# Attention and deformable convolution of 32 images on one core: another order of stages for ScalarE and VectorE, x loaded first, seam rows copied by ScalarE

## The chip, the cores and the metric

One core of one Trainium2 chip runs the whole program. The metric is the device time of one execution in microseconds, from three runs of the kernel before. All times below are microseconds (us) unless marked ns. The engines are TensorE (PE; its weight loads are shown as PEld), VectorE (DVE), ScalarE (ACT), GpSimd (POOL) and SyncE (SP), which only starts DMAs here; ScalarE starts some DMAs too.

## What is computed

The input x is 32 images of 192 channels and 32 x 32 positions in fp32. Two layers are added to it one after the other, each on a group-normalized input:

```python
def attention(x, w_qkv, w_out, b_out):              # B=32, C=192, N=1024
    q, k, v = split(einsum('bnc,dc->bnd', tokens(x), w_qkv))
    attn = softmax(einsum('bcn,bdn->bcd', q, k) * 48 ** -0.5)   # over channels
    return einsum('bnc,dc->bnd', attn @ v, w_out) + b_out

def deformable(x, ...):                             # 3 x 3 taps
    offset = clip(conv(x, off_w, off_b), -8, 8)     # 18 channels
    mask = 2 * sigmoid(conv(x, mask_w, mask_b))     # 9 channels
    y = deform_conv(x, offset, mask, proj_w, proj_b)     # bilinear samples
    return gelu(batchnorm(y) * gamma + beta)        # mean and variance over all images

x = x + attention(groupnorm(x))
x = x + deformable(groupnorm(x))
```

## The kernel before

**Two parts per image.** `part0` makes everything that an image needs before its deformable convolution, in stages with names: statistics of x (`x_stats`), `moments0`, `group0`, `rstd0`, the normalization (`norm0` to `norm3`, ScalarE) with its fp16 high and low parts (`low0` to `low3`, VectorE), the turning of x into tokens (`turn_x0` to `turn_x3`), the Gram matrix (`gram`), its products (`gram_wq`, `logits`), softmax over channels (`exp`, `prob`), `prob_wo`, `wv`, the product with x (`apply0` to `apply3`, which gives x1), then the same normalization of x1 (`moments1`, `group1`, `rstd1`, `norm4` to `norm7`, `low4` to `low7`) into the fp16 planes `x2`, the copies for taps that look left and right (`x2s`, by DMA), and from there offsets, mask and the bilinear weights ("hats") of rows (`rows`, `row_act`, `row_hats`) and of columns (`columns`, `column_hats`).

**`part1`** is the deformable convolution. It runs 48 units `u` per image. A unit on TensorE is: `turn_s(u+2)`, three fp32 transposes of a sampling matrix sT (line 765) into the PSUM banks `sps`; `convolve(u)`, nine fp16 products of sh and sl with zh and zl (lines 782 to 784); `z_group(u+10)`, five products of the projection weights with `x2` (lines 751 to 755) into `zps`. Each of the two PSUM results is cast to fp16 by ScalarE (`split_s` line 987, `split_z` line 963), and VectorE writes what the cast lost (lines 1266 and 1260). GpSimd makes sT as a product of row and column hats (line 1456), one for every two units. `turn_s(u)` waits until `split_s(u-2)` is done on VectorE; `z_group(g)` waits for `split_z(g-2)`. After every sixth unit ScalarE copies the finished accumulator y from `acc` into `ypm` (lines 1007 and 1008), and the next `convolve` waits for that copy. `TURN_Y` and `SCALE_Y` name the units at which y is turned and scaled.

**What sets the order.** Nothing is scheduled by a program. Every engine runs its own list in the order in which the code writes it. The table `PLAN` says beside which unit of `part1` of one image the stages of `part0` of the next image stand; numbers above 47 or below 0 spill into the neighbouring image. `beside` writes these stages at the end of a unit on each engine. So a stage that waits on an engine holds back all the casts behind it on that engine. Images come in a loop of two (`Fori`, line 391), with the first and the last three written out. For image 0 alone, `part0` is run with nothing beside it, and `part1` begins with ten `z_group`s.

**The start.** VectorE waits for the weights of the two convolutions, finds their largest magnitude, scales them to a power of two and splits them into fp16 high and low parts (lines 1035 to 1062), then begins with x. The three attention matrices follow at `turn_x3` (`weights_ready`). SyncE loads the convolution weights, then `eye`, x of image 0 and the tables `avg`, `cy`, `cx`.

**Between `low7` and the offsets.** SyncE starts six shifted copies x2 to x2s and two "seam" copies of three rows each into `x2w` (lines 506 and 507), which the `z_group`s of the first tile read. GpSimd waits for all eight, sets edge columns to zero (`edges`, line 1433) and raises `x2_moved`, on which both the offset convolution (line 694) and `z_group(0)` wait.

Of the kernel before, what the change touches and what calls it, by code (L numbers as in the profile page):

```python
# [35 lines left out]
P = 128  # L36
# [49 lines left out]
def build(nc, x, w_qkT, w_v, w_outT, b_out, w_off, b_off, w_proj, proj_b, gamma, beta,  # L86
# [6 lines left out]
    with ExitStack() as ctx:  # L93
# [33 lines left out]
        boff = sb("boff", [P, TILES, J])  # L127
# [111 lines left out]
        x2_shifted = sem("x2_shifted")  # L239
        edges_due = sem("edges_due")  # L240
# [46 lines left out]
        MATRIX_DMAS = TILES + 3 + 3 + 6 + 3 * 4  # L287
# [55 lines left out]
        def all_pairs(eng, step):  # L343
# [3 lines left out]
            for i in range(PAIRS - ROUND_ENDS):  # L347
# [33 lines left out]
        def images(program, eng):  # L381
# [3 lines left out]
            part0, part1, weights_ready = program  # L385
            for stage in STAGES:
                part0(stage, 0, 0)
                if stage == "turn_x3":
                    weights_ready()
# [25 lines left out]
        TURN_Y, SCALE_Y = (14, 25, 36), (16, 26, 37)  # L415
# [51 lines left out]
        def _(sp):  # L467
# [3 lines left out]

            load_blocks(sp, off_stage, w_off, weights_in)
# [3 lines left out]
            sp.dma_start(avg_sb[:, :, :], avg.rearrange("p (a b) -> p a b", a=4)).then_inc(const_in, 16)  # L476
            sp.dma_start(cy_sb[:, :], cy).then_inc(const_in, 16)
            sp.dma_start(cx_sb[:, :, :], cx.rearrange("p (k x) -> p k x", k=TAPS)).then_inc(const_in, 16)
# [15 lines left out]
            def shift(b, par):  # L494

                seam = lambda h: x2w_all[:, :, par, h * WRAP * W:(h + 1) * WRAP * W]
# [9 lines left out]
                sp.dma_start(seam(0), plane[:, :, N - WRAP * W:N]).then_inc(x2_shifted, 16)  # L506
                sp.dma_start(seam(1), plane[:, :, 0:WRAP * W]).then_inc(x2_shifted, 16)
# [78 lines left out]
        def _(pe):  # L586
            pe.wait_ge(const_in, CONST_DMAS * 16)
            pe.wait_ge(dve_setup, 2)
            pe.wait_ge(pool_setup, 1)

            for i in range(2):
                mm = pe.transpose(yt[:, i * P:(i + 1) * P], wmax[:, i:i + 1].broadcast_to([P, P]), eye32[:, :])
            mm.then_inc(pe_setup, 1)

            def weights_ready():
                pe.wait_ge(matrices_in, MATRIX_DMAS * 16)
                pe.wait_ge(dve_setup, 4)
                for i in range(3):
                    mm = pe.transpose(acc[:, i * P:(i + 1) * P], amax[:, i:i + 1].broadcast_to([P, P]), eye32[:, :])
                mm.then_inc(pe_setup, 1)  # L600
# [26 lines left out]
            def transpose_x(r, b):  # L627
                if r == 0:
                    pe.wait_ge(xn_lo, 8 * b + 4)
# [26 lines left out]
            def gram_times_wq(b):  # L656

                if first(b):
                    pe.wait_ge(dve_setup, 5)
# [168 lines left out]
            def part1(b, par, left, i=None):  # L828
                if first(b) or i is not None:
                    for g in range(AHEAD):  # L830
                        z_group(g, b, par)
                    turn_s(0, b)
                    turn_s(1, b)
# [21 lines left out]
            images((part0, part1, weights_ready), pe)  # L855
# [4 lines left out]
        def _(act):  # L860
# [9 lines left out]
            for t in range(TILES):  # L870
                act.dma_start(boff[:, t, :], b_off.partition_broadcast(P)).then_inc(matrices_in, 16)
            act.wait_ge(const_in, CONST_DMAS * 16)
            act.wait_ge(pool_setup, 1)

# [650 lines left out]
```

## Time and profile before

| | |
|---|---|
| time, median of 3 runs | 3814.17 us (3813.31 to 3821.13) |
| profiled execution | 3809.4 us, of which its span 3807.7 us |
| TensorE busy | 3417.3 us, 90% of the span |
| VectorE, ScalarE, GpSimd busy | 2609.9, 2127.9 and 1427.8 us |
| before the regular run of images | 0 to about 118 us |
| last stage (GELU and final sum, TensorE idle) | about 3592 to 3808 us |
| granted TensorE clock, mean | 0.965 |

The time divides into three stretches. In the first 118 us nothing overlaps, since image 0 is alone. From there to about 3580 us an image takes some 108.5 us and TensorE is busy nearly all of it. The last 216 us load, add and store all images and are bound by DMA. A wait in the rows below is told as "engine line waited for: us in total, times, longest"; in a timeline row the bracket is the idle time just before the instruction and what ended it.

### The profile page before, as it was taken

The numbers are of one execution on the slowest core, as the hardware profiler recorded it, in microseconds if no ns is written. First come the engines' busy times: TensorE is split into PE (matmuls) and PEld (weight loads), VectorE is DVE, ScalarE is ACT, GpSimd is POOL, SyncE is SP. The second block draws the span as 40 slices with busy tenths as digits, with TensorE's granted clock in tenths as the row PEclk, the third lists the DMA queues.
The fourth block names the chain that finished last, engine by engine and source line by source line (L and its number), as shares of the span: only waits on it lengthen the run. The fifth ranks groups of instructions, "written<-read, shape, count | busy, mean of one in ns | idle before, by whom it ended". The sixth has DMA issues, their size and how long they took to land.

```text
span 3807.7 us, 109692 instructions
## 1 busy us (share of the span) xinstructions
PE 3417.3 (90%) x38854; PEld 3019.7 (79%) x38854; DVE 2609.9 (69%) x5727; ACT 2127.9 (56%) x4854; POOL 1427.8 (37%) x1226
## 2 busy tenths in 40 slices
PE   2799999999999999999999999999999999999500
PEld 1688888888888888888888888888888888888500
DVE  4577777777777777777777777777777777776422
ACT  1465555655656556556565566565655665655332
POOL 1343433443434334334344343344433433444211
PEclk8999999999999999999999999999999999999855
DMA  2011111110111111101111111111111111011498
GB/s 68 18 48 48 40 48 48 48 35 28 43 48 39 48 48 47 35 30 41 47 40 48 47 48 37 33 35 48 40 47 48 47 41 34 31 47 36 138 368 298
DMA packets 104140, 225.31 MB, mean 59 GB/s; under 512 B 38432, under 2 KB 64288, under 8 KB 103584
## 3 DMA queue, kind: packets, MB, share of 16 engines
q1 hardware_dynamic: 92832, 191.76, 15.7%
q0 software_dynamic: 7168, 25.17, 1.7%
q8 instruction: 348, 5.70, 0.6%
q14 instruction: 208, 1.70, 0.2%
q10 hardware_dynamic: 3584, 0.97, 0.1%
HBM read 87.36 MB, written 75.50 MB: 43 GB/s over the span
## 4 chain that ended last, share of the span: by engine, by line
PE 76%; issue 6%; ACT 6%; DVE 5%; DMA 4%; ACTq 1%; DVEq 1%; SPq 1%; POOL 0%; POOLq 0%
PE sps L765 12%; PE acc L782 8%; PE acc L784 8%; PE acc L783 8%; PE l L694 5%; PE zps L755 4%; PE zps L751 4%; PE zps L754 4%; PE zps L752 4%; PE zps L753 4%; DMA xn<-x_scratch 2%; PE l L615 2%; DMA out<-x 1%; PE l L636 1%; DVE xhl_b L1133 1%
## 5 line engine op out<-in xcount | busy, mean ns | idle before, releaser
L1456 POOL TENSOR_TENSOR sT<-ay,bx 128x768 f32<-128x768 f32 x768 | 1140.3, 1493 | 1451.8 <-PE sps L765 1444.3
L782 PE MATMUL acc<-zh,sh 128*128 128x192 f16 x4608 | 1134.0, 246 | 28.2 <-ACT ypm L1008 28.2
L784 PE MATMUL acc<-zh,sl 128*128 128x192 f16 x4608 | 1133.6, 246 | 0.0
L783 PE MATMUL acc<-zl,sh 128*128 128x192 f16 x4608 | 1133.6, 246 | 0.0
L1266 DVE TENSOR_TENSOR sl<-sps,sh 128x384 f16<-128x384 f32 x1536 | 847.0, 552 | 349.3 <-ACT sh L987 328.1
L963 ACT CAST zh<-zps 128x288 f16<-128x288 f32 x1536 | 616.9, 402 | 711.9 <-PE zps L755 692.0
L987 ACT CAST sh<-sps 128x384 f16<-128x384 f32 x1536 | 738.5, 481 | 424.4 <-PE sps L765 413.2
L1260 DVE TENSOR_TENSOR zl<-zps,zh 128x288 f16<-128x288 f32 x1536 | 694.1, 452 | 341.6 <-ACT zh L963 333.6
L765 PE MATMUL sps<-eye,sT 128*128 128x128 f32 x4608 | 769.9, 276 | 10.1 <-issue 7.8
L765 PEld LDWEIGHTS sps<-eye,sT 128*128 128x128 f32 x4608 | 546.5, 141 | 81.6 <-issue 23.1
L782 PEld LDWEIGHTS acc<-zh,sh 128*128 128x128 f16 x4608 | 450.7, 98 | 40.3 <-ACT ypm L1008 33.9
L783 PEld LDWEIGHTS acc<-zl,sh 128*128 128x128 f16 x4608 | 450.9, 98 | 16.6
L784 PEld LDWEIGHTS acc<-zh,sl 128*128 128x128 f16 x4608 | 450.9, 98 | 0.0
L751 PE MATMUL zps<-wpr_h,x 128*128 128x288 f16 x1344 | 384.4, 286 | 0.5 <-DVE zl L1260 0.5
L752 PE MATMUL zps<-wpr_l,x 128*128 128x288 f16 x1344 | 384.4, 286 | 0.0
L753 PE MATMUL zps<-wpr_h,x 128*128 128x288 f16 x1344 | 384.4, 286 | 0.0
L754 PE MATMUL zps<-wpr_h,x 128*128 128x288 f16 x1344 | 384.4, 286 | 0.0
L755 PE MATMUL zps<-wpr_l,x 128*128 128x288 f16 x1344 | 384.4, 286 | 0.0
L1440 POOL TENSOR_TENSOR bx<-off,cx_sb 128x576 f32<-128x576 f32 x128 | 154.0, 1214 | 208.2 <-DVE off L1223 208.2
L694 PE MATMUL l<-wof,x2s 128*128 128x54 f16 x4608 | 186.6, 186 | 13.2 <-POOL x2s L1433 13.2
L694 PEld LDWEIGHTS l<-wof,x2s 128*128 128x128 f16 x4608 | 180.7, 96 | 16.3 <-POOL x2s L1433 13.3
L694 PE MATMUL l<-wof,x 128*128 128x54 f16 x2304 | 175.9, 186 | 0.0
(205 smaller groups left out, 5506.0 us busy)
## 6 DMA issues: line engine op xcount, KB each, us to landing
x2s<-x SPq DMA_DIRECT2D x192, 255.8 KB, 2.5
xin<-in_x SPq DMA_DIRECT2D x32, 512.0 KB, 5.2
xin<-in_x SPq DMA_DIRECT2D x64, 256.0 KB, 5.7
x_scratch<-x SPq DMA_DIRECT2D x32, 512.0 KB, 2.7
y_scratch<-ych SPq DMA_DIRECT2D x32, 512.0 KB, 2.7
zh<-y_scratch SPq DMA_DIRECT2D x20, 512.0 KB, 10.6
zl<-x_scratch SPq DMA_DIRECT2D x20, 512.0 KB, 11.4
out<-zh POOLq DMA_DIRECT2D x20, 512.0 KB, 8.8
```

The costliest lines, as they stand in the source:

```text
L694: mm = pe.matmul(o, src[:, row * W:(row + ROWS_T) * W], wof[:, m, k].rearrange("p i j -> p (i j)"), start=(k == 0 and n == 0), stop=(k == ...
L751: pe.matmul(o, at(0), wpr_h[:, 0, ky, n], start=True, stop=False)
L752: pe.matmul(o, at(0), wpr_l[:, 0, ky, n], start=False, stop=False)
L765: mm = pe.transpose(sps[u % 2][:, kx * P:(kx + 1) * P], sT[:, g, kx, c * P:(c + 1) * P], eye32[:, :])
L782: pe.matmul(acc[:, 0:C], s_h, zh[:, j, ky, z], start=start and kx == 0, stop=False)
L783: pe.matmul(acc[:, 0:C], s_h, zl[:, j, ky, z], start=False, stop=False)
L784: mm = pe.matmul(acc[:, 0:C], s_l, zh[:, j, ky, z], start=False, stop=stop and kx == 2)
L963: act.copy(z_piece(zh, g, par), zps[:, g % 2, 0:KO // 2]).then_inc(z_hi, 1)
L987: act.copy(sh[:, u % S_RING].rearrange("p k n -> p (k n)"), sps[u % 2][:, 0:3 * P]).then_inc(s_hi, 1)
L1260: dve.tensor_tensor(z_piece(zl, g, par), zps[:, g % 2, 0:KO // 2], z_piece(zh, g, par), ALU.subtract)\
L1266: dve.tensor_tensor(one(sl), sps[u % 2][:, 0:3 * P], one(sh), ALU.subtract).then_inc(s_lo, 1)
L1456: pool.tensor_tensor(sT[:, p % ST_RING].rearrange("p k (r x) -> p k r x", r=R), a, x_, ALU.mult)\
```

## The change

**The table.** In `PLAN`, `prob_wo` to `group1` move one unit later (16 to 17, ..., 24 to 25) and `rstd1` stands at 26 together with `norm4`. `norm6` and `norm7` move to 30 and 31, `low6` and `low7` to 32 and 33. A new stage `seams0` stands at 34. `rows1`, `row_act1` and `row_hats1` leave the table (44, 45, 46) and are done at units 7, 10 and 11 of the image's own `part1` (`ROWS_1`); `column_hats1` moves from 46 to 44. `TURN_Y` 25 becomes 26, `SCALE_Y` 16 and 26 become 17 and 27; column hats 2 move from unit 14 to 16; y's statistics and the offset distance move by one unit.

**Seams.** ScalarE copies the seam rows at `seams0` in two instructions, after waiting for `low7`. The two seam DMAs are gone, GpSimd waits for six copies, and `z_group(0)` waits for ScalarE (`seams_copied`) and no longer for `x2_moved`.

**Transposes.** `turn_x0` waits for the third low part (`low2`), `turn_x2` for the fourth.

**The start.** SyncE loads x of image 0 first, then the tables, then the weights. VectorE does all weight work inside `part0` of image 0: the maxima and the attention matrices behind `low3`, the scaling of the convolution weights behind `gram_wq0`, their splitting behind `prob0`. The bias `boff` is one DMA and not eight. ScalarE runs one tiny activation as soon as the constants are there. Behind `edges0`, five of the ten first `z_group`s are done, before the offset convolution.

```diff
-        MATRIX_DMAS = TILES + 3 + 3 + 6 + 3 * 4
+        MATRIX_DMAS = 1 + 3 + 3 + 6 + 3 * 4
...
-                21: ("apply3",), 22: ("moments1",), 24: ("group1",), 25: ("rstd1",), 26: ("norm4",),
+                22: ("apply3",), 23: ("moments1",), 25: ("group1",), 26: ("rstd1", "norm4"), 27: ("norm5",),
...
-            load_blocks(sp, off_stage, w_off, weights_in)
-            load_blocks(sp, proj_stage, w_proj, weights_in)
-            sp.dma_start(eye32[:, :], eye).then_inc(const_in, 16)
-            load_x(0)
...
+            load_x(0)
+            sp.dma_start(avg_sb[:, :, :], avg.rearrange("p (a b) -> p a b", a=4)).then_inc(const_in, 16)
...
+            load_blocks(sp, off_stage, w_off, weights_in)
             load_blocks(sp, proj_stage, w_proj, weights_in)
...
-                sp.dma_start(seam(0), plane[:, :, N - WRAP * W:N]).then_inc(x2_shifted, 16)
-                sp.dma_start(seam(1), plane[:, :, 0:WRAP * W]).then_inc(x2_shifted, 16)
...
+                if stage == "edges0":
+                    pe.wait_ge(dve_setup, 4)
+                    for g in range(AHEAD // 2):
+                        z_group(g, 0, 0)
...
-                if r == 0:
-                    pe.wait_ge(xn_lo, 8 * b + 4)
+                if r % 2 == 0:
+                    pe.wait_ge(xn_lo, 8 * b + 3 + r // 2)
...
                 if g == 0:
-                    pe.wait_ge(x2_moved, b + 1)
+                    pe.wait_ge(seams_copied, b + 1)
...
+            act.activation(gb[:, :], mhalf[:, :], ACT.Identity, scale=mhalf[:, 0:1], bias=mhalf[:, 1:2])
...
+                if name == "seams":
+                    act.wait_ge(xn_lo, 8 * b + 8)
+                    for h, row in ((0, H - WRAP), (1, 0)):
+                        at = (PAD_T + row) * W
+                        ins = act.copy(x2w_all[:, :, par, h * WRAP * W:(h + 1) * WRAP * W],
+                                       x2_all[:, :, par, at:at + WRAP * W])
+                    ins.then_inc(seams_copied, 1)
...
-                    if u in (14, 24):
-                        column_hats((14, 24).index(u) + 2, b, par)
+                    if u in (16, 24):
+                        column_hats((16, 24).index(u) + 2, b, par)
+                    if u == ROWS_1[1]:
+                        row_act(1, b, par)
...
+            def first_image(stage):
+                if stage == "low3":
+                    largest_weights()
+                    split_matrices()
+                    powers_of_two(scale[:, :], unscale[:, :], wmaxt[:, :])
+                if stage == "gram_wq0":
+                    for w, shaped, w_h, w_l, i in splits:
+                        dve.tensor_scalar(w, w, scale[:, i:i + 1], None, ALU.mult)
+                if stage == "prob0":
+                    for w, shaped, w_h, w_l, i in splits:
+                        dve.tensor_copy(w_h, shaped)
...
-                pool.wait_ge(x2_shifted, 128 * b + 128)
+                pool.wait_ge(x2_shifted, 96 * b + 96)
```

How the instructions stand before and after is shown at three places. **The start, on VectorE.** `zh` and `zl` hold the raw convolution weights there, `ych` the attention matrices. Before, the program begins so:

```order
L1036 TENSOR_REDUCE wmaxt<-zh 128x1 [waits weights_in]
L1036 TENSOR_REDUCE wmaxt<-zl 128x1
L1038 TENSOR_SCALAR cmid<-cy_sb 128x1 [waits const_in]
...
L1055 TENSOR_SCALAR zl<-zl,scale 128x1728 x2
...
L1061 TENSOR_TENSOR wpr_l<-zl,wpr_h 128x1728 x2
L1106 BN_STATS stats<-xin 128x6 [waits x_loaded] x4
```

After the change:

```order
L1053 TENSOR_SCALAR cmid<-cy_sb 128x1 [waits const_in]
L1054 CAST eye<-eye 128x128
L1122 BN_STATS stats<-xin 128x6 [waits x_loaded] x4
...
L1158 TENSOR_TENSOR xhl_b<-xn,xhl_b 64x512 [waits xn_hi] x2
L1071 TENSOR_REDUCE wmaxt<-zh 128x1 [waits weights_in]
L1071 TENSOR_REDUCE wmaxt<-zl 128x1
...
L1125 SCALAR_TENSOR_TENSOR t_l<-l_1,t_h 64x192
L1106 TENSOR_SCALAR zh<-zh,scale 128x243 x2
L1106 TENSOR_SCALAR zl<-zl,scale 128x1728 x2
L1200 TENSOR_REDUCE nmax<-l_0 128x1 [waits log_ps]
```

The statistics of x now stand ahead of all weight work, and the weight work stands in three pieces behind stages of image 0. **Beside units 13 to 17, on ScalarE**, in a written-out image whose order is that of the loop; bx are the column hats. Before:

```order
L954 ACTIVATE bx<-bx 128x576 [waits dx_sb]
L956 ACTIVATE bx<-bx 128x576
L963 CAST zh<-zps 128x288 [waits z_ps,sz_done]
L987 CAST sh<-sps1 128x384 [waits sz_done,s_ps]
L963 CAST zh<-zps 128x288 [waits z_ps]
L987 CAST sh<-sps0 128x384 [waits sz_done,s_ps]
L963 CAST zh<-zps 128x288 [waits z_ps]
L891 ACTIVATE rmat_h<-l0_1 128x192 [waits r_ps]
```

After the change:

```order
L979 CAST zh<-zps 128x288 [waits z_ps,sz_done]
L1003 CAST sh<-sps1 128x384 [waits sz_done,s_ps]
L979 CAST zh<-zps 128x288 [waits z_ps]
L1003 CAST sh<-sps0 128x384 [waits sz_done,s_ps]
L970 ACTIVATE bx<-bx 128x576 [waits dx_sb]
L972 ACTIVATE bx<-bx 128x576
L979 CAST zh<-zps 128x288 [waits z_ps]
L1003 CAST sh<-sps1 128x384 [waits sz_done,s_ps]
L1025 COPY ypm<-acc 128x192 [waits yt_ps,sz_done]
```

The pair on bx stands two units later, and the copy of y now comes ahead of rmat_h (`prob_wo`). **Beside units 33 to 35, on ScalarE**, in the same image. Before:

```order
L987 CAST sh<-sps0 128x384 [waits sz_done,s_ps]
L963 CAST zh<-zps 128x288 [waits z_ps]
L987 CAST sh<-sps1 128x384 [waits sz_done,s_ps]
L1007 COPY ypm<-acc 128x192 [waits yt_ps,sz_done]
L1008 COPY ypm<-acc 128x64
```

After the change:

```order
L1003 CAST sh<-sps0 128x384 [waits sz_done,s_ps]
L979 CAST zh<-zps 128x288 [waits z_ps]
L949 COPY x2w<-x2 128x3x96 [waits xn_lo]
L949 COPY x2w<-x2 128x3x96
L1003 CAST sh<-sps1 128x384 [waits sz_done,s_ps]
L1025 COPY ypm<-acc 128x192 [waits yt_ps,sz_done]
L1026 COPY ypm<-acc 128x64
```

The two seam copies, with their wait for the last low part, stand ahead of a cast of s and of a copy of y.

## Rows read from the trace of the kernel before

**Rows 1.** Waits of PE in 220 to 3472 us (thirty images): total, times, longest.
```profile
PE acc L782 <- ACT ypm L1008: 26.7, 47, 1.0
PE l L636 <- DVE xhl_b L1133: 24.3, 30, 0.9
PE sps L765 <- issue: 7.8, 13, 0.9
PE l L615 <- DVE prob_l L1095: 7.0, 30, 0.2
```

**Rows 2.** Timeline of PE: start, us, instruction, idle time before; the waits of one image.
```profile
1342.03 0.23 PE L636 MATMUL l<-eye,xh_a 128*128 128x128 f16 x1 [0.81 <-DVE xhl_b L1133]
1367.56 0.26 PE L615 MATMUL l<-wo_h,prob_h 128*128 128x192 f16 x1 [0.24 <-DVE prob_l L1095]
1399.57 0.26 PE L782 MATMUL acc<-zh,sh 128*128 128x192 f16 x1 [0.57 <-ACT ypm L1008]
1437.70 0.26 PE L782 MATMUL acc<-zh,sh 128*128 128x192 f16 x1 [0.52 <-ACT ypm L1008]
```

**Rows 3.** Timeline of DVE, POOL and ACT around the softmax of one image.
```profile
1360.73 1.40 DVE L1180 TENSOR_TENSOR nmaxs<-nmax,log_scale 128x1 f32<-128x1 f32 x2
1365.65 0.16 DVE L1184 RECIPROCAL rinv<-rsum 128x2 f32<-128x2 f32 x1
...
1360.56 1.48 POOL L1456 TENSOR_TENSOR sT<-ay,bx 128x768 f32<-128x768 f32 x1 [5.34 <-PE sps L765]
1364.36 1.48 POOL L1456 TENSOR_TENSOR sT<-ay,bx 128x768 f32<-128x768 f32 x1 [1.21 <-PE sps L765]
...
1363.51 0.69 ACT L954 ACTIVATE bx<-bx 128x576 f32<-128x576 f32 x1
```

**Rows 4.** Timeline of DVE and ACT around the last low part and the copy of y.
```profile
1405.69 1.20 DVE L1133 TENSOR_TENSOR x<-xn,x 64x512 f16<-64x512 f32 x1
...
1409.01 0.32 ACT L1007 COPY ypm<-acc 128x192 f32<-128x192 f32 x1 [0.26 <-PE acc L784]
```

**Rows 5.** Timeline of DVE and PE in the stage of image 0 alone.
```profile
16.28 0.66 DVE L1036 TENSOR_REDUCE wmaxt<-zh 128x1 f32<-128x486 f32 x1 [16.28 <-DMA zl<-in_w_proj]
16.85 3.74 DVE L1036 TENSOR_REDUCE wmaxt<-zl 128x1 f32<-128x3456 f32 x1
23.02 0.15 DVE L1038 TENSOR_SCALAR cmid<-cy_sb 128x1 f32<-128x1 f32 x1 [2.42 <-DMA cx_sb<-in_cx]
25.88 2.15 DVE L1055 TENSOR_SCALAR zl<-zl,scale 128x1728 f32<-128x1728 f32 x2
28.09 0.72 DVE L1058 CAST wof<-zh 128x243 f16<-128x243 f32 x2
35.21 2.46 DVE L1106 BATCH_NORM_STATS2 stats<-xin 128x6 f32<-128x512 f32 x4
50.20 2.00 DVE L1069 TENSOR_REDUCE amax<-ych 128x1 f32<-128x768 f32 x3
59.99 0.47 DVE L1095 SCALAR_TENSOR_TENSOR gram<-l,gram 128x192 f16<-128x192 f32 x2
66.28 0.61 DVE L1175 TENSOR_REDUCE nmax<-l 128x1 f32<-128x192 f32 x2 [2.58 <-PE l L617]
73.36 0.61 DVE L1095 SCALAR_TENSOR_TENSOR rmat_l<-l,rmat_h 128x192 f16<-128x192 f32 x2 [3.15 <-ACT rmat_h L891]
```

**Rows 6.** The chain that ended last: last low parts and offset convolution of image 0.
```profile
96.01 1.30 DVE x L1133 x2
102.50 7.72 PE l L694 x216
```

**Rows 7.** Timeline of ACT: last hats of image 0, first and last of ten z casts.
```profile
115.14 0.44 ACT L945 ACTIVATE ay<-ay 128x288 f32<-128x288 f32 x1 [0.64 <-DVE ay L1227]
117.33 0.68 ACT L963 CAST zh<-zps 128x288 f16<-128x288 f32 x2
...
126.18 0.40 ACT L963 CAST zh<-zps 128x288 f16<-128x288 f32 x1 [0.64 <-PE zps L755]
```

More of the change, by code:

```diff
@@ L587, in _ @@
             pe.wait_ge(const_in, CONST_DMAS * 16)
-            pe.wait_ge(dve_setup, 2)
+            pe.wait_ge(dve_setup, 1)
             pe.wait_ge(pool_setup, 1)
[L591 to L600, printed above, removed]
+            def first_image(stage):
+                if stage == "turn_x3":
+                    pe.wait_ge(dve_setup, 2)
+                    for i in range(5):
+                        column = wmax[:, i:i + 1] if i < 2 else amax[:, i - 2:i - 1]
+                        at = yt[:, i * P:(i + 1) * P] if i < 2 else acc[:, (i - 2) * P:(i - 1) * P]
+                        mm = pe.transpose(at, column.broadcast_to([P, P]), eye32[:, :])
+                    mm.then_inc(pe_setup, 1)
+                if stage == "edges0":
+                    pe.wait_ge(dve_setup, 4)
+                    for g in range(AHEAD // 2):
+                        z_group(g, 0, 0)
             def group_stats(n, b):
@@ L829, in part1 @@
                 if first(b) or i is not None:
-                    for g in range(AHEAD):
+                    for g in range(AHEAD // 2 if i is None else 0, AHEAD):
                         z_group(g, b, par)
@@ L990, in part1 @@
                 if first(b) or i is not None:
-                    for g in range(AHEAD):
+                    for g in range(AHEAD // 2 if i is None else 0, AHEAD):
                         split_z(g, b, par)
@@ L1032, in _ @@
         def _(dve):
-            dve.wait_ge(weights_in, 6 * 16)
-            for i, stage in enumerate((off_stage, proj_stage)):
-                dve.tensor_reduce(wmaxt[:, i:i + 1], stage, AX.XY, ALU.max, apply_absolute_value=True)
             dve.wait_ge(const_in, CONST_DMAS * 16)
@@ L1092, in weights_ready, with first_image, channel_stats @@
                 ins.then_inc(dve_setup, 1)
+            def first_image(stage):
+                if stage == "low3":
[8 more added lines that the diff above has]
+                        dve.tensor_copy(w_h, shaped)
+                    dve.drain()
+                    for w, shaped, w_h, w_l, i in splits:
+                        ins = dve.tensor_tensor(w_l, shaped, w_h, ALU.subtract)
+                    ins.then_inc(dve_setup, 1)
+                    dve.wait_ge(dve_setup, 4)
+                if stage == "edges0":
+                    for g in range(AHEAD // 2):
+                        split_z(g, 0, 0)
+            def channel_stats(q, src):
+                i, half = divmod(q, 2)
+                dve.bn_stats(stats[:, i, half], src[:, i, half * 512:half * 512 + 512])
             def low_part(dst, src, by, hi):
@@ L1336, in part1 @@
                 if first(b) or i is not None:
-                    for g in range(AHEAD):
+                    for g in range(AHEAD // 2 if i is None else 0, AHEAD):
                         split_z(g, b, par)
@@ L1369, in part1 @@
                     y_stats(3, b, par)
-            images((part0, part1, weights_ready), dve)
+            images((part0, part1, first_image), dve)
             def again():
@@ L1463, in part1 @@
                     beside(part0, u, b, par, left)
-            images((part0, part1, lambda: None), pool)
+            images((part0, part1, lambda stage: None), pool)
             where_far(pool, lambda: once_more(
```

138 lines of the change are left out of this document (67 added, 71 removed), and 8 rows, old and new, of the table PLAN.

## The prediction, made before the changed kernel was run

> **What bounds the kernel now.** I read the page first: TensorE is busy 90% of the span, and its idle time lies at both ends. Then the waits of TensorE over thirty regular images [rows 1]: they add up to 65.8 us, so whatever the change does there, it can give back about 2 us per image. Of that, 7.8 us stand as "issue", which the profile ties to no other engine; it occurs every second image only, and I leave it alone. The timeline shows where the others sit [rows 2]. The first transposes of x wait 0.81 for the last low part, in all 30 images. `prob_wo` waits 0.24 for `prob`. `convolve` of unit 30 waits 0.57 for the copy of y, and `convolve` of the next image's unit 0 waits 0.52 for it in the images without the issue wait; 47 such waits are 30 of the first kind and 17 of the second. The second view is the timeline of the stage in which image 0 is alone [rows 5 to 7]; there every microsecond of the chain counts once. The last stage (216 us, bound by DMA) is not touched, and I carry it over.
>
> **Start: x ahead of the weights.** The statistics of x begin at 35.21 [rows 5], behind a wait for the tables that ends at 23.02 and 12.2 us of weight work. Now they begin when x and the tables have landed. The weights, first in the queue, landed at 16.28 with about 2.0 MB; x and the tables have 1.5 MB (both by their shapes). In proportion that is 12 to 13 us, and I take 12.5, with 10 to 15 as bounds. From statistics to the end of the low parts nothing changes (35.21 to 50.20, 15.0 us), so `low3` ends at 27.5, by which time the weights and matrices are there. Then:
> - From 50.20 to the low part of the Gram matrix at 59.99 are 9.8 us: maxima of the three matrices, their turning, the split. Now the maxima of the convolution weights come in too, 0.66 + 3.74 overlapping to 4.3, and for two more maxima 0.8 in small instructions and turning, an estimate. `gram` is then at 27.5 + 9.8 + 4.3 + 0.8 = 42.4, **17.6 us sooner**.
> - Scaling the weights (28.09 less 0.6 ahead of 25.88, 2.8 us) stands ahead of the maximum of the logits, where VectorE idled 2.58: costs 0.2.
> - Splitting them (28.09 to 35.21, 7.1 us) stands ahead of the low part of rmat, where VectorE idled 3.15: **costs 4.0**.
> - From the last low part's end (96.01 + 1.30 = 97.3) to the offset convolution at 102.50 [rows 6] TensorE waited for DMAs and GpSimd. Five `z_group`s now stand there. Ten of them took 117.33 to 126.18 for nine steps [rows 7], 0.98 each, so seam copies and five groups need about 6 us: the convolution starts 0.8 later, but on an engine that has just worked. It took 7.72 for 216 products; I take 5.9 to 7.7, a gain of 1.0 net.
> - After the offsets, the second row half no longer stands ahead of the z casts (115.14 less its 0.64 of idle, to 116.00: 1.5 us), and five of nine steps are gone (4.4): **5.9 sooner**.
> Sum: 17.6 - 0.2 - 4.0 + 1.0 + 5.9 = **20.3 us**, bounds 15 and 25. ScalarE's table load moves off the chain too, worth at most 1.3, within these bounds.
>
> **Transposes on the third low part.** TensorE was ready 0.81 before 1342.03. Two low parts take 1.30 back to back [rows 6], 0.65 each, and here VectorE has two casts' remainders between the third and the fourth (about half a microsecond each, an estimate), so the third is done over 1 us earlier and the whole wait goes: **24.3 us** in thirty images. Nothing is behind it: the next transposes wait for ScalarE as before.
>
> **ScalarE's heavy stages off y's copies.** `norm6` stood a unit ahead of the copy after unit 29, now it stands behind it: 30 x 0.57 = 17.1. `column_hats1` and `row_act1` leave units 45 and 46: the other 17 waits, 26.7 - 17.1 = 9.6, go. `row_act1` now costs ScalarE 0.9 (two of 0.44 [rows 7]) at unit 10, where TensorE has the whole Gram product behind the unit, and VectorE's two row instructions fall into idle time beside units 7 and 11: nothing. Together **26.7 us**.
>
> **`prob_wo` one unit later, column hats from unit 14 to 16.** The wait of 0.24 goes (7.0 us). But what stood between was a cushion. `prob` ran from 1365.65 to about 1367.5 [rows 2, 3]. Without the pair of column hats (two of 0.69) ahead of it on ScalarE it could begin at 1364.5. GpSimd's sT runs there, 1364.36 to 1365.84. In the same image `nmaxs`, a one-column instruction, took 1.3 of the 1.40 of its pair because sT ran from 1360.56; it ended with sT. So `prob`, apart from its reciprocal, is held to 1365.84 and ends at 1367.4 as before. Behind it VectorE has the remainder of s for unit 17 (some 0.55, an estimate), until 1368.0. `turn_s(19)` waits for that, and TensorE, which no longer has `prob_wo` to do at unit 16, is free for it at 1367.3 (1367.56 less the 0.24). A new wait of 0.7, bounds 0 and 1.0: **costs 30 x 0.69 = 20.7**, so the edit costs 13.7 net.
>
> The Trainium skill, page "SBUF — State Buffer", section "Who interferes with whom", says that GpSimd and VectorE share one pair of ports, whole instruction by whole instruction, and that not only instructions with two SBUF inputs but also a `tensor_scalar` in a 2-port mode take it. By that rule both high parts of `prob` are held, as in my sum; if only two-input instructions were, the wait would be near nothing, which is rival B below. The trace agrees for two inputs (`nmaxs`).
>
> **Seam copies on ScalarE.** The trace has no such copy. Its nearest rows are a copy of 192 columns, 0.32 [rows 4], and a cast of 288 columns, 0.40 [rows 7]; two of 288 overlapping make 0.7, bounds 0.6 and 1.6. They stand ahead of the cast of s for unit 37 and of the copy of y after unit 35, and wait for `low7`. `low7` stood at 1405.69 and took 1.20 since an sT held it; a unit later (1.7) it runs free and ends near 1407.8. The copy of y has 0.26 of idle ahead of it [rows 4] and gets behind by 0.6, so `convolve` of unit 36 waits 0.35, bounds 0.1 and 1.3: **costs 30 x 0.35 = 10.5**. The seam DMAs that go were on no path of TensorE in a regular image. `x2_moved` comes earlier relative to `low7`, and `low7` is a unit later: nothing.
>
> **Sum.** Thirty images: 24.3 + 26.7 + 7.0 - 20.7 - 10.5 = 26.8, with image 0 as a thirty-first 27.7. With the start: 20.3 + 27.7 = 48.0 of 3809.4 in the profiled execution, 3761.4. The median of the runs is 4.8 above that execution, so the prediction for the median is **3766**.
>
> **Rivals.**
> - B, no collision at `prob`: VectorE's five instructions run beside sT, `turn_s(19)` does not wait. For it: `prob` was never seen beside sT. Against: `nmaxs`. 31 x 0.69 = 21.4 less: 3745.
> - C, the seam copies cost 0.9 more per image, because they are slow or `low7` is held by sT after all: 31 x 0.9 = 28 more, 3794. The same number comes out if other small waits arise at stages that now meet another neighbour. For it: sT held `low7` and others in the trace; against: sT of that time waits behind `edges`.
> - D, the landing of x and tables is not sooner than 20 us, since ScalarE's loads share the engines: 7.5 us less gain, 3773.
> - E, slower: `low7`, seam copies, cast and copy of y are one chain through two engines at unit 35. Beyond my 0.35 each further microsecond counts fully, thirty-one times; the gain of 48 is gone at 1.55 more per image, and at 1.9 more (copies of 0.8 each, and `low7` a whole sT later) it is 31 x 1.9 - 48 = 11 slower, 3825. It decides only beyond both bounds above together.
>
> **How the numbers follow.** Forecast 0.50, B 0.20, C 0.18, D 0.07, not faster by the change of order at all 0.03 (3810), E 0.02. The range takes in B, C and D with the bounds of the start: 3736 to 3796. A measurement of this kernel tells about 0.2% (8 us) from no change. Faster by more than that: 0.95; within: 0.03; slower: 0.02.
>
> **What would show it.** The statistics of x begin near 12.5, the tenth z cast ends near 106 and not 126. TensorE's wait at the transposes of x is gone; no wait of unit 30 for y; a new wait of 0.7 at sps behind the remainder of s, and one of 0.35 at acc behind the copy of y, each about thirty times. `prob`'s instructions end with sT. It is wrong if the new waits are more than two, or if the images do not come 0.9 closer together.

## The result and the profile after

| | before | after |
|---|---|---|
| median of the runs | 3813.74 us (4 runs, 3804.66 to 3821.13) | 3750.34 us (4 runs, 3740.71 to 3751.09) |
| ratio, 95% interval | | 0.9824, 0.9808 to 0.984 |
| profiled execution | 3809.4 us | 3751.09 us |
| begin of the Gram product of image 1 (TensorE) | 156.37 us | 134.01 us |
| from one Gram product to the next, regular image without a back edge | 108.53 us | 106.91 us |

The change gives 63.4 us where 48.0 were forecast. The time lies inside the range (3736 to 3796), on its lower side. Where it came from is seen in a table of stretches, cut at the begin of image 1's Gram product, at that of the last image, and at TensorE's end. Columns: stretch, its length, busy time and number of instructions of TensorE, its weight loads, VectorE, ScalarE, GpSimd, then the granted clock, the share of the DMA engines, GB/s. Before:

```profile
0.00:156.00 156.00, 69.68 (x696) 52.59 (x696) 71.42 (x157) 44.62 (x85) 34.39 (x33) 0.86 0.20 52
156.00:3413.00 3257.00, 3185.28 (x36382) 2820.77 (x36383) 2369.89 (x5275) 1932.84 (x4494) 1292.24 (x1079) 1.00 0.13 42
3413.00:3579.00 166.00, 162.32 (x1778) 146.32 (x1776) 106.61 (x240) 88.00 (x224) 65.46 (x49) 1.00 0.12 37
3579.00:3807.70 228.70, 0.00 (x0) 0.00 (x0) 61.98 (x58) 62.48 (x53) 35.70 (x65) 0.51 0.93 325
```

After:

```profile
0.00:134.00 134.00, 71.50 (x696) 53.84 (x696) 70.88 (x157) 46.02 (x88) 34.06 (x33) 0.82 0.21 59
134.00:3350.00 3216.00, 3178.40 (x36384) 2825.09 (x36385) 2416.02 (x5270) 1951.19 (x4552) 1284.31 (x1079) 1.00 0.13 41
3350.00:3515.00 165.00, 162.03 (x1777) 146.25 (x1774) 109.11 (x245) 89.50 (x228) 65.13 (x49) 1.00 0.12 38
3515.00:3749.40 234.40, 0.00 (x0) 0.00 (x0) 61.78 (x57) 62.48 (x53) 35.82 (x65) 0.51 0.93 317
```

The start is 22 us shorter, the thirty images 41, the last one 1. The last stage, whose code is the same, took 5.9 longer in this execution, counted from TensorE's end (229 us before, where I had put 216; 227 to 241 us in the executions profiled below, over all kernels). TensorE is therefore done 64.2 sooner (3578.45 against 3514.23), while the two profiled executions differ by 58.3 only. In the thirty images VectorE is busy 46 us longer with the same work, because other instructions of it now take longer, among them the scaling in `prob` (30 x 0.97 = 29 us more, looked at below) and the offset distance (`ypos`, 53.6 us and not 14.3). Only the first has a wait of TensorE behind it.

**The regular images.** The waits of TensorE from 200 to 3412 us, in the columns of [rows 1]:

```profile
PE sps L765 <- DVE sl L1295: 22.8, 41, 1.1
PE acc L782 <- ACT ypm L1026: 9.3, 30, 0.4
PE l L615 <- DVE rmat_l L1125: 0.4, 1, 0.4
```

Of the four rows in [rows 1] those for the low parts (24.3) and for `prob` (7.0) are gone, the one for y fell from 26.7 in 47 waits to 9.3 in 30, and one at `sps` is new. It holds two things. Thirty of its 41 waits are of 0.5 and stand 17.7 us behind the Gram product; a timeline there:

```profile
1326.14 1.48 POOL L1489 TENSOR_TENSOR sT<-ay,bx 128x768 f32<-128x768 f32 x1 [1.20 <-PE sps L765]
...
1326.27 0.15 DVE L1209 RECIPROCAL rinv<-rsum 128x2 f32<-128x2 f32 x1
...
1326.51 1.14 DVE L1211 TENSOR_SCALAR rinv<-rinv 128x2 f32<-128x2 f32 x1
...
1327.72 0.54 DVE L1215 TENSOR_SCALAR prob_h<-xt,rinv 128x192 f16<-128x192 f32 x2
...
1328.35 0.74 DVE L1125 SCALAR_TENSOR_TENSOR prob_l<-xt,rinv,prob_h 128x192 f16<-128x192 f32 x2
...
1329.01 0.54 DVE L1295 TENSOR_TENSOR sl<-sps,sh 128x384 f16<-128x384 f32 x1
...
1329.61 0.55 PE L765 MATMUL sps<-eye,sT 128*128 128x128 f32 x3 [0.51 <-DVE sl L1295]
```

This is the collision of the forecast. The scaling of two numbers takes 1.14 us and ends at 1327.65, just behind sT (1327.62); the reciprocal ahead of it, also inside sT, takes 0.15. `prob` ends at 1329.09, the remainder of s behind it at 1329.55, and TensorE starts 0.06 later.

The wait for y stands at unit 36 alone:

```profile
1369.23 0.69 DVE L1158 TENSOR_TENSOR x<-xn,x 64x512 f16<-64x512 f32 x1
...
1369.96 0.76 ACT L949 COPY x2w<-x 128x288 f16<-128x288 f16 x2 [0.35 <-DVE x L1158]
...
1371.00 0.32 ACT L1025 COPY ypm<-acc 128x192 f32<-128x192 f32 x1
...
1371.21 0.23 ACT L1026 COPY ypm<-acc 128x64 f32<-128x64 f32 x1
...
1371.49 0.26 PE L782 MATMUL acc<-zh,sh 128*128 128x192 f16 x1 [0.30 <-ACT ypm L1026]
```

`low7` runs free (0.69), the pair of seam copies takes 0.76, and behind it come the cast of s and the copy of y.

**The end of the loop body.** The other 11 waits at `sps` stand 87 to 88 us behind the Gram product, at the end of the loop body's second image. The fourteen passes of the loop have 13 back edges, so two are without such a wait. The row puts them down to VectorE:

```profile
1504.36 0.56 DVE L1295 TENSOR_TENSOR sl<-sps,sh 128x384 f16<-128x384 f32 x1
...
1505.20 0.55 DVE L1295 TENSOR_TENSOR sl<-sps,sh 128x384 f16<-128x384 f32 x1
...
1506.73 0.54 PE L765 MATMUL sps<-eye,sT 128*128 128x128 f32 x3 [1.14 <-DVE sl L1295]
```

Both remainders had ended by 1505.75, 0.98 before TensorE went on. The kernel before has the same gap in the same place, 0.84 there and called "issue":

```profile
1546.22 0.54 PE L765 MATMUL sps<-eye,sT 128*128 128x128 f32 x3 [0.84 <-issue]
```

**The start.** VectorE's rows of image 0 (below them the last z cast on ScalarE), to be read against [rows 5, 7]:

```profile
11.31 2.46 DVE L1122 BATCH_NORM_STATS2 stats<-xin 128x6 f32<-128x512 f32 x4
...
23.68 1.29 DVE L1158 TENSOR_TENSOR xhl_b<-xn,xhl_b 64x512 f16<-64x512 f32 x2 [0.97 <-ACT xhl_b L885]
...
25.58 3.74 DVE L1071 TENSOR_REDUCE wmaxt<-zl 128x1 f32<-128x3456 f32 x1
...
39.65 0.48 DVE L1125 SCALAR_TENSOR_TENSOR gram<-l,gram 128x192 f16<-128x192 f32 x2
...
46.88 0.61 DVE L1200 TENSOR_REDUCE nmax<-l 128x1 f32<-128x192 f32 x2
...
54.11 3.82 DVE L1112 TENSOR_TENSOR wpr_l<-zl,wpr_h 128x1728 f16<-128x1728 f32 x2
...
57.96 0.61 DVE L1125 SCALAR_TENSOR_TENSOR rmat_l<-l,rmat_h 128x192 f16<-128x192 f32 x2
...
80.54 1.29 DVE L1158 TENSOR_TENSOR x<-xn,x 64x512 f16<-64x512 f32 x2 [0.97 <-ACT x L885]
...
104.11 0.40 ACT L979 CAST zh<-zps 128x288 f16<-128x288 f32 x1 [0.80 <-PE zps L755]
```

And the five z groups and the offset convolution, as stretches (columns as above):

```profile
82.70:88.30 5.60, 5.53 (x27) 3.21 (x28) 1.47 (x4) 1.60 (x4) 0.94 (x2) 0.55 0.25 94
88.30:93.90 5.60, 5.60 (x219) 5.58 (x218) 0.83 (x3) 0.40 (x1) 0.00 (x0) 1.00 0.02 6
```

The groups run at a granted clock of 0.55, the lower of the two levels (1.2 GHz) in the main; the convolution behind them at 1.00 (2.4 GHz) and in 5.60 us. Before, it began on an idle engine and took 7.72 [rows 6].

### The profile page after: what moved, and what is told of

It is laid out like the page before. It is cut to its first block, busy times and chain, and to the rows that moved or that the text cites. A ratio compares the mean times of both kernels' runs of the same rounds, so it can differ in the third digit from the quotient of the medians.

```text
span 3749.4 us, 109745 instructions
## 1 busy us (share of the span) xinstructions
PE 3411.9 (91%) x38854; PEld 3025.2 (81%) x38854; DVE 2657.8 (71%) x5727; ACT 2149.2 (57%) x4919; POOL 1419.3 (38%) x1226
## 4 chain that ended last, share of the span: by engine, by line
PE 82%; DVE 4%; DMA 4%; ACT 3%; issue 3%; DVEq 1%; ACTq 1%; SPq 1%; POOL 0%; POOLq 0%
PE sps L765 13%; PE acc L782 9%; PE acc L784 9%; PE acc L783 9%; PE l L694 5%; PE zps L755 4%; PE zps L751 4%; PE zps L753 4%; PE zps L754 4%; PE zps L752 4%; DMA xn<-x_scratch 3%; PE l L615 2%; DMA out<-x 2%; PE l L636 1%; PE l L617 1%
```

## The experiments

Each kernel is the changed one with the edit shown. "Period" is the distance between two Gram products in regular images that have no wait at the back edge; it repeats within 0.01 us and is therefore a finer measure than the time. Medians with an interval are from three or more rounds against the kernel before, whose median was 3812.89 to 3816.21 us in them.

| kernel | median, us | ratio to before (95%) | image 1 begins | period |
|---|---|---|---|---|
| before | 3813.74 | | 156.37 | 108.53 |
| changed kernel | 3750.34 | 0.9808 to 0.984 | 134.01 | 106.91 |
| start alone | 3799.66 | 0.993 to 0.997 | 139.10 | 108.51 |
| `prob` at 15 | 3731.39 | 0.9768 to 0.9801 | 133.37 | 106.17 |
| column hats at 14 | 3758.86 | 0.9838 to 0.9871 | 132.34 | 107.09 |
| seam copies at 35 | 3733.65 | 0.9776 to 0.9809 | 133.34 | 106.43 |
| four images in the loop | 3747.32 | 0.9804 to 0.9837 | 133.90 | 106.91 |
| splitting spread | 3747.72 | 0.9806 to 0.9838 | 129.10 | 106.91 |
| fourth low part | 3782.6, one run | | 133.38 | 107.88 |
| seam copies twice | 3775.6, one run | | 133.25 | 107.73 |
| three edits | 3711.37 | 0.9713 to 0.9753 | 128.36 | 105.70 |
| five edits | 3705.82 | 0.9699 to 0.9726 | 126.94 | 105.69 |
| seams by DMA | 3726.7, one run | | 137.83 | 106.43 |
| weights first | 3765.4, one run | | 142.65 | 106.91 |

**Start alone.** The table, `TURN_Y`, `SCALE_Y`, the second row half, column hats, seams and transposes are those of before; of that edit the core:

```diff
-                34: ("seams0",), 36: ("edges0",),
+                32: ("low7",), 36: ("edges0",),
...
-                    pe.wait_ge(seams_copied, b + 1)
+                    pe.wait_ge(x2_moved, b + 1)
...
-                if r % 2 == 0:
-                    pe.wait_ge(xn_lo, 8 * b + 3 + r // 2)
+                if r == 0:
+                    pe.wait_ge(xn_lo, 8 * b + 4)
```

> Only the changes of the start are in this kernel (x and tables loaded ahead of the weights, weight work inside image 0, one DMA for the bias, table load moved, five z groups ahead of the offset convolution). The table of stages, the seam DMAs and the wait of the transposes are those of the kernel before. Theory 1 (the surplus over the forecast lies in the thirty images): a regular image takes 108.5 us as before, the Gram product of image 1 begins some 21 to 22.5 us sooner than 156.4, and the median is 21 to 23 below that of before, about 3791 to 3793. Rival (the surplus of 10 to 15 us lies in the start and the first images): 30 to 35 below, about 3781. A gain under 18 would say that the new order has its share in the first image.

It gained 16.5 (3816.21 to 3799.66), and image 1 begins 17.3 sooner. My theory said 21 to 22.5, so it missed, and so did the rival with 30 or more: the surplus is not in the start. Image 1 begins 5.1 us later than in the changed kernel. Three of them are in this row:

```profile
85.78 0.40 PE L754 MATMUL zps<-wpr_h,x2w 128*128 128x288 f16 x1 [13.27 <-POOL x2s L1469]
```

Without ScalarE's copies, z group 0 waits for `x2_moved` (GpSimd's edge columns), so the five groups stand ahead of the convolution on the chain and not beside the DMAs: they begin at 85.78 and not at 82.78. Another 1.6 us lie between the end of the convolution and the last z cast (11.9 and not 10.3). The second row half, which this kernel leaves where it was, stands ahead of the casts there again, so my 21 to 22.5 counted a gain that this kernel does not have.

**`prob` beside unit 15.**

```diff
-                10: ("gram0",), 11: ("gram_wq0",), 12: ("logits0",), 13: ("exp0",), 14: ("prob0",),
+                10: ("gram0",), 11: ("gram_wq0",), 12: ("logits0",), 13: ("exp0",), 15: ("prob0",),
```

> The changed kernel with stage prob beside unit 15 and not 14, nothing else. Theory 1 (prob's instruction on two sums is held by GpSimd's product sT, which runs from 14.2 to 15.7 us after the start of the Gram product): at unit 15 prob meets no sT, its second instruction takes about 0.17 us and not 1.14, TensorE's wait for the remainder of s (0.5 in the row) falls to 0.2 or less, a regular image takes 106.3 to 106.5 and not 106.9, and the time is 11 to 17 below the changed kernel, about 3736. Rival (VectorE simply has too much to do in two units, whoever holds it): the wait moves by a unit and stays 0.4 to 0.6, 106.9 per image, about 3750.

```profile
1322.01 0.17 DVE L1211 TENSOR_SCALAR rinv<-rinv 128x2 f32<-128x2 f32 x1
```

and from its waits of TensorE, 220 to 3400 us:

```profile
PE sps L765 <- DVE sl L1295: 8.0, 10, 1.1
```

The same instruction, one unit later and beside no sT, takes 0.17. The thirty waits are gone, only ten at the back edge are left in the row, and the period falls by 0.74, more than I expected: 19 us, by one number in the table. VectorE's load is the same, so the rival falls.

**Column hats 2 beside unit 14.**

```diff
-                    if u in (16, 24):
-                        column_hats((16, 24).index(u) + 2, b, par)
+                    if u in (14, 24):
+                        column_hats((14, 24).index(u) + 2, b, par)
```

> The changed kernel with the pair of column hats 2 back beside unit 14, nothing else. Theory 1: prob then starts about 1 us later, behind sT, and its instructions run unheld; it ends some 0.2 us later than in the changed kernel, so TensorE's wait behind it is 0.5 to 0.8 in the row and an image takes 106.9 to 107.2: about 3750 to 3758. That is, moving the hats was worth nearly nothing, since the collision ate it. Rival (the later hats do free prob and the wait of 0.5 is only what is left): with the hats back the wait is longer by the pair, 1.2 or more, an image takes 107.6 or more, about 3770.

```profile
1325.14 1.48 POOL L1489 TENSOR_TENSOR sT<-ay,bx 128x768 f32<-128x768 f32 x1 [1.21 <-PE sps L765]
...
1326.66 0.17 DVE L1211 TENSOR_SCALAR rinv<-rinv 128x2 f32<-128x2 f32 x1
...
1328.80 0.55 PE L765 MATMUL sps<-eye,sT 128*128 128x128 f32 x3 [0.70 <-DVE sl L1295]
```

`prob` now comes behind sT, runs free, and ends no sooner: TensorE waits 0.70 and not 0.51, the period is 0.18 longer. Taking the pair of hats (1.4 us) out of its way was worth 0.18.

**Seam copies beside unit 35**, behind the copy of y:

```diff
-                34: ("seams0",), 36: ("edges0",),
+                35: ("seams0",), 36: ("edges0",),
```

> The changed kernel with the seam copies beside unit 35 and not 34, so that they stand behind ScalarE's copy of y and not ahead of it. Theory 1: the wait of 0.31 at acc goes (0.36 from start to start), no other arises, since the next cast of s had 0.4 us of idle and its remainder is wanted a unit later; an image takes 106.5 to 106.6, about 3740. Rival (the seam copies cost wherever they stand, because ScalarE has 0.76 more to do): a wait of about the same size at sps or zps one or two units on, 106.9 per image, about 3750.

```profile
PE sps L765 <- DVE sl L1295: 19.9, 37, 1.1
PE l L615 <- DVE rmat_l L1125: 0.4, 1, 0.4
```

The row at `acc` is gone, nothing takes its place, and the period falls by 0.48, where I had put the wait at 0.36 from start to start: that value was too small. It was the place of the copies, not the work.

**Four images in the loop.**

```diff
-            with nc.Fori(1, NB - 4, 2, engines=[eng.engine], hint_back_edge=True) as b:
-                part1(b, 1, 2)
-                part1(b + 1, 0, 2)
+            with nc.Fori(1, NB - 4, 4, engines=[eng.engine], hint_back_edge=True) as b:
+                for n in range(4):
+                    part1(b + n, 1 - n % 2, 2)
```

> The changed kernel with four images in the loop and not two: seven back edges and not fourteen, the order of all instructions otherwise the same. The wait in question is TensorE's at sps, 87 to 88 us after the start of the Gram product, in 11 of the images at the end of the loop body, 0.4 to 1.3 each; the trace puts it down to VectorE's remainder of s. Theory 1 (it is the back edge of the loop, as the issue wait was before, and VectorE had ended before): it now comes at every fourth image only, at most 7 times, and the time is 3 to 6 shorter, 3744 to 3747. Rival (VectorE is late there, as the row says): it stays at every second image and nothing changes, 3750.

```profile
PE sps L765 <- DVE sl L1295: 15.4, 30, 0.5
PE acc L782 <- ACT ypm L1026: 8.9, 29, 0.4
PE acc L784 <- issue: 3.2, 1, 3.2
```

(Waits of TensorE from 220 to 3400 us, as in the other experiments below and above.) Exactly the thirty waits behind `prob` are left at `sps`, at 0.5 each; the 11 are gone, also at the six back edges that remain. So they belong to the loop and not to VectorE, and 22.8 - 15.4 = 7.4 us of the row were wrongly labelled. But one stall of 3.2 is new, in the first `convolve` behind the loop's exit, and that image takes 111.93: 3.4 later through the stall, and 1.7 more because the granted clock behind it is 0.66 from 3217 to 3222 us (1.00 ahead of it). The median gained 3 us (3750 to 3747), within what the measurement can tell. Why the shorter body has no such stall at its exit stays open.

**Splitting of the weights spread** over VectorE's idle time:

```diff
-                if stage == "gram_wq0":
+                if stage == "gram0":
                     for w, shaped, w_h, w_l, i in splits:
                         dve.tensor_scalar(w, w, scale[:, i:i + 1], None, ALU.mult)
-                if stage == "prob0":
+                if stage == "gram_wq0":
+                    dve.drain()
                     for w, shaped, w_h, w_l, i in splits:
                         dve.tensor_copy(w_h, shaped)
+                if stage == "prob0":
                     dve.drain()
-                    for w, shaped, w_h, w_l, i in splits:
+                    for w, shaped, w_h, w_l, i in splits[:3]:
+                        dve.tensor_tensor(w_l, shaped, w_h, ALU.subtract)
+                if stage == "prob_wo0":
+                    for w, shaped, w_h, w_l, i in splits[3:]:
                         ins = dve.tensor_tensor(w_l, shaped, w_h, ALU.subtract)
```

> The changed kernel with the work on the convolution weights in image 0 put into VectorE's idle stretches: scaling behind gram0, the high parts behind gram_wq0, three of the four low parts behind prob, the last one behind prob_wo. Theory 1 (the splitting in one piece holds the low part of rmat, 4.0 us as forecast): the low part of rmat begins at 53.9 to 54.5 and not 57.96, TensorE's wait for it falls from 5.3 to 1.3 to 1.9, image 1 begins 3.5 to 4.2 sooner (129.8 to 130.5), and the time is about 3746. Rival (what follows is bound by something else, for example by the offset convolution's DMAs): image 1 begins less than 1 sooner, 3750.

```profile
53.46 0.61 DVE L1130 SCALAR_TENSOR_TENSOR rmat_l<-l,rmat_h 128x192 f16<-128x192 f32 x2 [0.46 <-ACT rmat_h L898]
```

The low part of rmat begins 4.5 sooner (57.96 to 53.46), and image 1 4.3 sooner than in the other kernels with the changed start (129.10 against 132.3 to 134.0, mostly some 133.4; the changed kernel itself 134.01). In the median it is 2.6, under what can be told.

**Fourth low part.**

```diff
-                if r % 2 == 0:
-                    pe.wait_ge(xn_lo, 8 * b + 3 + r // 2)
+                if r == 0:
+                    pe.wait_ge(xn_lo, 8 * b + 4)
```

> The changed kernel with the transposes of x waiting for the fourth low part again. Theory 1 (this wait is worth in the changed order what it was before, 0.81 in the row, 0.97 from start to start): an image takes 107.8 to 107.9, in all 29 to 30 us longer, about 3780. Rival (the later stages around it moved, so that part of the wait would have gone anyway): 107.4 or less, 3765.

```profile
PE l L636 <- DVE xhl_b L1158: 24.3, 30, 0.9
```

The old row is back to the tenth (24.3 in 30), and the period grows by 0.97, not by the 0.81 of the row. That difference is looked at below.

**Seam copies twice**, the same two again behind a drain of ScalarE:

```diff
+                    act.drain()
+                    act.copy(x2w_all[:, :, par, 0:WRAP * W], x2_all[:, :, par, PAD_T * W + (H - WRAP) * W:PAD_T * W + H * W])
+                    ins = act.copy(x2w_all[:, :, par, WRAP * W:2 * WRAP * W], x2_all[:, :, par, PAD_T * W:(PAD_T + WRAP) * W])
                     ins.then_inc(seams_copied, 1)
```

> The changed kernel with the two seam copies done twice, one after the other (the same rows again), beside unit 34. Theory 1 (copies, cast of s and copy of y are one chain, and beyond it each further microsecond counts fully): 0.76 more work and a drain of ScalarE make the wait at acc 1.1 to 1.2 and not 0.31, an image takes 107.7 to 107.8, about 25 us longer in all, 3775. Rival (ScalarE's idle time takes it up): wait under 0.7, less than 10 us longer.

```profile
PE acc L782 <- ACT ypm L1029: 32.8, 29, 1.2
```

The waits grow from 0.31 to 1.13 each, the period by 0.82, for 0.76 of copies and the drain. It is one chain and each further microsecond counts: rival E's mechanism is right, though its size never came about.

**Three edits, and five.** The three are `prob` at 15, seam copies at 35, splitting spread; the other two are the loop of four and a call of `largest_conv`, the first half of `largest_weights` (maxima of the convolution weights, with their wait), ahead of the low parts:

```diff
+                if stage == "norm1":
+                    largest_conv()
                 if stage == "low3":
                     largest_weights()
```

> Three edits together on the changed kernel: prob beside unit 15, seam copies beside unit 35, splitting of the convolution weights spread over VectorE's idle stretches. Theory 1 (the three waits are separate, so the gains add): 0.74 and 0.48 less per regular image give 105.7, image 1 begins at about 129, no wait of TensorE is left in a regular image but the one at the back edge; 28 x 1.22 + 4.2 = 38 below the changed kernel, about 3711 to 3716. Rival (ScalarE or VectorE is next in line once both waits are gone): 106.0 or more per image, 3722 or more.

> As the kernel with the three edits, and two more: four images in the loop, and in image 0 the maxima of the convolution weights taken ahead of the low parts, where VectorE waits for ScalarE. Theory 1: the waits at the back edge go and one stall of some 5 us at the loop's exit comes (2 to 5 less in all); the low part of the Gram matrix begins 3 us sooner. Together 4 to 8 below that kernel, 3705 to 3710. Rival (the stall at the exit eats what the edges give, and the maxima meet another wait): within 2 of it.

The gains add: 0.74 + 0.48 = 1.22, and the period is 105.70 (1.21 less). With the five edits there is no wait in a regular image, and TensorE's waits from 220 to 3380 us are two (the stall behind the loop's exit, and one in the last images):

```profile
PE acc L784 <- issue: 2.9, 1, 2.9
PE l L615 <- DVE prob_l L1134: 0.7, 1, 0.7
```

The maxima ahead of the low parts gave 1.4 and not 3 (low part of the Gram matrix at 37.83, in the kernel with three edits at 39.21): the weights had landed at 20.5 only, and the low parts waited for the maxima until 24.74. The kernel with five edits takes 3705.82, 44.5 below the changed one; against the one with three (3711.37) it is at the edge of what can be told.

**Seams by DMA**, as before the change:

```diff
-                34: ("seams0",), 36: ("edges0",),
+                36: ("edges0",),
...
+                sp.dma_start(seam(0), plane[:, :, N - WRAP * W:N]).then_inc(x2_shifted, 16)
+                sp.dma_start(seam(1), plane[:, :, 0:WRAP * W]).then_inc(x2_shifted, 16)
...
-                    pe.wait_ge(seams_copied, b + 1)
+                    pe.wait_ge(x2_moved, b + 1)
...
-                pool.wait_ge(x2_shifted, 96 * b + 96)
+                pool.wait_ge(x2_shifted, 128 * b + 128)
```

> The changed kernel with the seam rows copied by DMA again (as before, so that z_group(0) waits for x2_moved), nothing else. Theory 1 (the copies by ScalarE pay only in image 0, where they let five z groups run while the shifted copies are under way, and cost in each regular image): image 1 begins 4 to 6 later, at 138 to 139; a regular image takes 106.4 to 106.5; in all 7 to 10 shorter, about 3742. Rival (the seam DMAs cost in regular images too, since z_group(0) or the offset convolution waits for them): 106.9 or more, 3755 or more.

It was better than I expected. Image 1 begins 4.4 later than in its neighbours (137.83 against 133.4), the period is 106.43, TensorE is done at 3497.81 and not 3514.23. Of these 16.4 us, some 6 are fewer waits at the back edge (they vary from kernel to kernel, 4 to 13 us in all), and the execution, the only one, has a short last stage (227 us). The rival's mechanism shows in two of the thirty images, in which `z_group(0)` waits 0.4 and 0.2 for `x2_moved`. So at unit 34 this part of the change costs some 10 us net; at unit 35 it gives the 4.4 of image 0 for nothing.

**Weights first**, in SyncE's queue alone:

```diff
+            load_blocks(sp, off_stage, w_off, weights_in)
+            load_blocks(sp, proj_stage, w_proj, weights_in)
             load_x(0)
...
             sp.dma_start(cx_sb[:, :, :], cx.rearrange("p (k x) -> p k x", k=TAPS)).then_inc(const_in, 16)
-            load_blocks(sp, off_stage, w_off, weights_in)
-            load_blocks(sp, proj_stage, w_proj, weights_in)
```

> The changed kernel with SyncE loading the convolution weights ahead of x and the tables again, nothing else; VectorE's order is that of the changed kernel. Theory 1 (the statistics of x wait for x and the tables alone): they begin at 19 to 20 and not 11.3, all of it counts, image 1 begins 7.5 to 9 later, about 3759. Rival (what counts is when the matrices have landed, 21.8, so the load order is worth little): less than 4 later, 3753.

```profile
21.25 2.46 DVE L1122 BATCH_NORM_STATS2 stats<-xin 128x6 f32<-128x512 f32 x4
```

The statistics begin 9.9 later and image 1 some 9 later (142.65 against 133.4 to 134.0), a little more than I expected. The load order is thus about two fifths of the 22.4 by which image 1 came sooner.

## Why the prediction was right, and where it was off

**The start: 20.3 forecast, 22.1 measured** to the end of the z casts (126.18 to 104.11), step by step:
- Statistics at 11.31 against 12.5: 1.2 more, by shapes and a proportion from one landing. From there to the end of `low3` 13.7 us and not 15.0: the difference is ScalarE's table load, left out of the sum as "at most 1.3": before, it took 1.28 between `nbias` and the first normalization (from 42.91); now it runs at 16.01, and the normalization at 19.01 waits for `nbias` alone. The low part of the Gram matrix came 20.3 sooner, not 17.6.
- Scaling: from that low part to the maximum of the logits 7.2 us against 6.3 before, so it cost 0.9 and not 0.2.
- Splitting: from there to the low part of rmat 11.08 against 7.08. It cost 4.0, as forecast; spreading it gave it back.
- Five groups and the offset convolution: 12.0 from the last low part to its end against 12.9, a gain of 0.9 (1.0 forecast). The convolution took 5.60, below the lower bound.
- After the offsets: 10.3 against 16.0, 5.7 sooner (5.9).

**The transposes and y's copies** went as said, all of them. **The collision at `prob`** came in every image, so rival B is out; `prob` at 15 and the column hats at 14 show it from both sides. The Trainium skill, page "SBUF — State Buffer", section "Who interferes with whom", counts a `tensor_scalar` among the instructions that can take the shared ports; the trace agrees for one on two numbers (1.14 us beside sT, 0.17 without). A reciprocal was not held (0.15). Both high parts of `prob` began only behind sT (1327.72 against 1327.62), so whether they would be held no run here shows. **The seam copies**: 0.35 forecast, 0.30 in the row; a pair took 0.76 for the 0.7. Rivals C, D and E did not come.

**The step that was off** is the unit of the sum for regular images. I took idle times from rows as the price of a wait, for the removed waits and for the new ones (the 0.69 at `sps` too, which counts from the end of TensorE's last instruction, 1367.3). The price is larger. Three edits on single waits measure it in the period: 0.97 for an idle time of 0.81 (fourth low part), 0.74 for 0.51 (`prob` at 15), 0.48 for 0.30 (seam copies at 35). The reason stands in the rows, here of TensorE where nothing waits, from the kernel with four images in the loop:

```profile
3212.31 0.29 PE L755 MATMUL zps<-wpr_l,x 128*128 128x288 f16 x1
3212.43 0.49 PE L765 MATMUL sps<-eye,sT 128*128 128x128 f32 x3
3212.76 0.25 PE L782 MATMUL acc<-zh,sh 128*128 128x192 f16 x1
```

Each row begins 0.16 to 0.17 before the one ahead of it ends. An idle time is counted from that end, so it leaves out these 0.16 which the wait also takes away. The three fp32 transposes of s take 0.55 behind a wait and 0.49 else, which is 0.06 more there.

With these prices the sum closes. The kernels with three and five edits run the same products without a wait in a regular image, in a period of 105.70. Before, the period was 2.83 above that, for 2.13 of idle time: 0.97 for the low part and 1.86 for `prob_wo` and the two waits for y together, where the forecast had 0.81 and 1.33. After the change it is 1.21 above, for 0.81 of idle time; 0.74 + 0.48 = 1.22 by the experiments. So the period fell by 1.62, where the terms of the forecast give 2.14 - 1.04 = 1.10. Of the 0.52 between them, 0.69 are the removed waits, priced too low, less 0.40 for the new waits, priced too low as well; the other 0.23 are new waits shorter than forecast. The one at `sps` was idle for 0.51 and not 0.69, because `prob` ended 1.47 behind sT and not 1.6, and the remainder of s 0.46 behind `prob` and not 0.6; the one at `acc` for 0.30 and not 0.35.

Over 29 intervals that is 1.62 x 29 = 47.0, less 8.6 that come back at the ends of the loop body and in the last image: before, the issue wait stood in place of the wait for y of unit 0 there, and it stayed. 38.4 were measured, where the forecast had 0.89 x 29 = 25.9. These 12.5 us, with 2.7 more in the first two images and 1.0 in the last one, are the surplus of 16.2 at TensorE's end. The forecast had allowed for the issue wait, by counting 17 waits for y of unit 0 and not 30. The errors in price of the removed and of the new waits have opposite signs in the sum, so they cancelled in part, which was luck.

## What to carry to other kernels

Price every wait in one measure, best the distance between two starts of the same instruction in neighbouring rounds; idle times leave out the overlap that a wait takes away (0.16 here) and make removed waits look cheap. Where VectorE and GpSimd meet in a fixed pattern, moving a stage by one unit can be worth more than taking work out of its way (0.74 against 0.18 per image here), and work moved to an engine with idle time belongs behind, not ahead of, the copy for which the bottleneck waits. A wait that the trace gives to an engine whose instruction had long ended is something else; where it stands in the loop tells more than its label.

## What was not expected of the hardware

- With two images in the loop, TensorE stood 0.2 to 1.2 us idle at 7 to 13 of the 13 back edges (with the seams by DMA at 3); with four images (six back edges) at none, but 3.2 and 2.9 us once, in the first `convolve` behind the exit, in both kernels with that loop. The cause is open.
- The last stage, bound by DMA and unchanged, took 227 to 241 us from one execution to another, more than most edits here are worth. The distance of starts in the regular images repeated within 0.01 us.
- The offset convolution ran 216 products in 5.6 us at a granted clock of 1.00 right behind five groups at 0.55; begun on an idle engine it took 7.7 at 0.69 on average.
